# Writing the zeros of a scatter buffer in HBM earlier, from an SBUF region of their own

## The chip, the core and the metric

One Trainium2 core of eight on its chip runs the program; the others are idle. The metric is the device time of one execution in microseconds (us), as a median over runs. Everything is float32 at the borders; inside, many matmuls split a factor into a rounded high part (fp32r) and the low rest, so that one product is three matmuls.

## The reference

Three blocks act on x, 8 x 64 tokens of 512 features, with residuals:

```python
x = x + xattn(layernorm(x), ctx_1024, ...)   # scores of 64 tokens against 512 context rows, softmax,
                                             # concat [c, c2q, c*c2q, c*q2c] @ W_l.T + b_l
x = x + attn(layernorm(x), ...)              # qkv, causal attention (16 heads of 32, S = 64),
                                             # conv of width 3 over tokens gives new queries,
                                             # attention again, out projection
x = x + ffn(layernorm(x), ...)               # 14 experts, top 2 of a softmax gate,
                                             # gelu(x @ w1[e] + b1[e]) @ w2[e] + b2[e], weighted sum
```

The last block is sparse here: each token's normed row is scattered to the rows of its two experts in an HBM buffer, each block of 128 rows is multiplied with its expert's weights, and the results are gathered back. Rows of a block that no token fills must hold zeros, so the buffer is cleared first.

## The kernel before

The 512 tokens are four tiles (n = 0..3, NT = 4) of 128 (P). The program is one block with a list of instructions for each engine; the order on an engine is the order in which they are written, and semaphores tie the engines together. There are three stages. The first is the cross attention with its projection, some 106 us long: a loop `for n in range(1, NT)` on ScalarE (ACT), VectorE (DVE) and TensorE (PE), whose pass n finishes the scores of tile n and starts those of tile n + 1 (`exp_scores(n + 1)`). The second is the small attention: `fill` pieces (projections of q, k, v and, later, the convolution) are woven on PE between `scores(m, half)`, `values(m)` (transposes of probabilities) and `outputs(m)`, m = 0..7 being two rounds over the four tiles. The third are the experts, with a loop over pairs of blocks.

What the change touches:

- `rows_dram` is the HBM buffer, 57 blocks (ROW_BLOCKS) of 128 rows of 512 floats: 14,592 KB. It is cleared by one DMA whose source is `zero_rows`, a 128 x 512 tile of zeros read 57 times. Before, `zero_rows` is another name for `att`, the tile into which the first stage's `exp_scores` writes and which later holds rows of the scatter's helper matrices (`spread`).
- `zero_made` tells that the tile holds zeros, `rows_zeroed` reaches 16 when the DMA has landed. GpSimd (POOL) fills the tile at L835, once the first stage is over (`z_psum` at NT); ACT issues the DMA at L658 to L661, behind `copy_cT(1, NT - 1)`. DVE waits for `rows_zeroed` ahead of `spread(0)` (L1376, it is the first that overwrites `att`), POOL ahead of the scatter.
- `A2` (its rounded view is `A2r`) is a region that changes its use with the stages. In the second stage, `o_hi` lies at columns 6144 and up: it holds the first attention's outputs with a border of zeros ("pads") that POOL writes at L834; DVE fills it in `take_out(m)` (L1162, and L1170 for the low rest `o_lo`). In the first stage, columns 3584 to 7680 hold the split parts.
- POOL's set-up in the second stage runs from L834 to L840: pads, three iotas (`slot_row_made`, for which DVE waits at L1333), pads of `o_lo`. Behind it stands `norm_probabilities(m)` (L823), for which `values(m)` on PE waits.
- On PE, the fill `("conv", 0, 0)` (L1683 to L1685) waits for `o_low` at 8, that is for the end of `take_out(1)` on DVE, and stands right behind `scores(3, 0)` and `scores(3, 1)` (L1704 and L1715).
- SyncE (SP) issues nearly all other loads. Around the change: context rows of tile 3 (L376), `conv` and `wo` (L402, L403) once the first stage is over, copies of v between halves (L408), then the first experts' weights (L413 to L415).

Of the kernel before, what the change touches and what calls it, by code (L numbers as in the profile page):

```python
# [23 lines left out]
P = 128  # L24
B, S = 8, 64
D = 512
Q = 512
KT = D // P
N = B * S
NT = N // P  # L30
# [7 lines left out]
ROW_BLOCKS = E + E * MORE + 1  # L38
# [10 lines left out]
def perceiver_kernel(nc, t, out):  # L49

    ctx = ExitStack()
    with ctx:
        def sb(name, shape, dt=F32):
            return ctx.enter_context(nc.sbuf_tensor(name, shape, dt))

        def overlaid(name, rounded_name, shape):

            with nc.sbuf_tensor(name, shape, F32) as plain:
                pass
            return plain, sb(rounded_name, shape, F32R)  # L60

        def sem(name):
            return ctx.enter_context(nc.semaphore(name))


        rows_dram = nc.dram_tensor("rows_dram", [ROW_BLOCKS * P, D], F32).ap()
# [60 lines left out]
        last_w = wqkv_flat[:, 4096:4608].rearrange("p (t s) -> p t s", t=NT)  # L127
        last_wT = wqkv_flat[:, 5120:5632].rearrange("p (t n) -> p t n", t=NT)
        A2, A2r = overlaid("A2", "A2r", [P, 3 * KT * N + KT * B * (S + 2)])
        cwT = A2[:, 0:2048].rearrange("p (k n) -> p k n", k=KT)  # L130

        c2qT, ccT, cqT = (A2[:, at:at + D].rearrange("p (k n) -> p k n", k=KT) for at in (2048, 2560, 3072))
# [23 lines left out]
        hpre = A2[:, 2048:3072]  # L156
        hT = A2[:, 3072:5120].rearrange("p (u f n) -> p u f n", u=2, f=FT)
        ysb = A2[:, 5120:6144].rearrange("p (u d) -> p u d", u=2)
        att = sb("att", [P, Q]); zero_rows = att

        attT = sb("attT", [P, KT, P]); c2q = sb("c2q", [P, D])
        slot_row_i = c2q[:, 0:P].bitcast(I32); last_w2 = c2q[:, P:2 * P]
# [110 lines left out]
        zero_made, rows_zeroed = sem("zero_made"), sem("rows_zeroed")  # L273
# [22 lines left out]
        def tile(n):  # L296
            return slice(n * P, (n + 1) * P)
# [8 lines left out]
        def out_bank(w):  # L306

            return TB if w else PO
# [5 lines left out]
        def piece(*what):  # L314

            return FILLS.index(what)
# [6 lines left out]
        def pieces(part, n):  # L323

            return parts_ahead[:, n - 1] if part == 0 and n else parts[:, part]

        def source(part, n):

            return (cT[:, :, tile(n)], c2qT, ccT, cqT)[part]
# [5 lines left out]
        def sixth_hi(i):  # L335

            return qkv_hi[i // 2][:, :, D * (i % 2) // 2:D * (i % 2 + 1) // 2]
# [136 lines left out]
        def _(act):  # L474
# [8 lines left out]
            def copy_cT(l, n):  # L483
                act.wait_ge(cT_psum, NT * l + n + 1)
                nc.scalar.activation((c_hi if l == 1 else cT)[:, :, tile(n)], turn_bank(l, n)[:, :].rearrange(
                    "p (k n) -> p k n", k=KT), ACT.Copy).then_inc(cT_ready, 1)
# [14 lines left out]
            def high_part(part, n):  # L501

                if part == 0:
                    act.wait_ge(cT_ready, n + 1)
                elif part == 1:
                    act.wait_ge(c2qT_ready, n + 1)
                elif part == 2:
                    act.wait_ge(cc_ready, n + 1)
                    if n:
                        act.wait_ge(z_psum, n)  # L510
                else:
                    act.wait_ge(cqT_ready, n + 1)
                nc.scalar.activation(pieces(part, n)[:, 0], source(part, n), ACT.Copy).then_inc(part_high[part], 1)

            def exp_scores(n):
                act.wait_ge(nmax_ready, n + 1)
                if n:
                    act.wait_ge(aT_psum, n)
                nc.scalar.activation(att[:, :], SC[:, :], ACT.Exp, bias=nmax[:, n:n + 1],
                                     accum_out=asum[:, n:n + 1]).then_inc(exp_done, 1)  # L520

            def turn_weights(n):

                act.wait_ge(aT_psum, n + 1)
                if n:
                    act.wait_ge(cq_psum, n)
                nc.scalar.activation(attT[:, :, :], TR[:, :].rearrange("p (k n) -> p k n", k=KT),
                                     ACT.Copy).then_inc(aT_ready, 1)

            def exp_maxima(n):  # L530

                act.wait_ge(msub_ready, n + 1)
                nc.scalar.activation(mT[:, :, :], mT[:, :, :], ACT.Exp).then_inc(mexp_done, 1)

            def copy_c2qT(n):

                act.wait_ge(c2qT_psum, n + 1)
                nc.scalar.activation(c2qT, TR[:, :].rearrange("p (k n) -> p k n", k=KT),
                                     ACT.Copy).then_inc(c2qT_ready, 1)

            def high_qkv(i):

                if i == 0:
                    act.wait_ge(wqkv_in, 16)
                    act.wait_ge(first_psum, NT)
                elif i == 4:
                    act.wait_ge(z_psum, NT)
                nc.scalar.activation(sixth_hi(i), wqkv[:, :, sixth(i)], ACT.Copy).then_inc(qkv_high, 1)
# [22 lines left out]
            for n in range(1, NT):  # L571
                turn_weights(n)
                high_part(2, n - 1)
                exp_maxima(n)
                if n == 2:
                    for i in range(4):
                        high_qkv(i)
                copy_c2qT(n)
                high_part(1, n)
                high_part(3, n)  # L580
                if n >= 2:
                    copy_cT(1, n - 2)
                if n + 1 < NT:
                    exp_scores(n + 1)
            high_part(2, NT - 1)

            def take(g):
# [55 lines left out]
            def exp_logits(n):  # L643
# [12 lines left out]
            take(2)  # L656
            take(3)
            copy_cT(1, NT - 1)  # L658
            act.wait_ge(zero_made, 1)
            act.dma_start(rows_dram.rearrange("(b p) d -> p b d", p=P),  # L660
                          zero_rows[:, :].unsqueeze(1).to_broadcast([P, ROW_BLOCKS, D])).then_inc(rows_zeroed, 16)  # L661
            take(piece("v", 0))
            exponentials(0)
            take(piece("qk", 1, 0))
# [120 lines left out]
        def _(pool):  # L785
# [21 lines left out]
            pool.wait_ge(consts, CONSTS - 1)  # L807
            nc.gpsimd.iota(over_row_i[:, :], pattern=[[1, OVER]], base=1, channel_multiplier=0).then_inc(consts, 1)

            pool.wait_ge(s_psum, 1)  # L810
            for dst, src in ((qkv_b, "qkv_bT"), (conv_b, "conv_bT")):
                pool.dma_start(dst[:, :], t[src]).then_inc(params_in, 16)
# [15 lines left out]
            for i in range(4, 6):  # L828
                pool.wait_ge(qkv_high, i + 1)
                nc.gpsimd.tensor_tensor(wqkv_lo[:, :, sixth(i)], wqkv[:, :, sixth(i)],  # L830
                                        sixth_hi(i).bitcast(F32), ALU.subtract).then_inc(pool_low, 1)
            pool.wait_ge(z_psum, NT)
            for side in (0, S + 1):
                nc.gpsimd.memset(o_hi[:, :, :, side:side + 1].bitcast(F32), 0.0).then_inc(pads_ready, 1)  # L834
            nc.gpsimd.memset(zero_rows[:, :], 0.0).then_inc(zero_made, 1)  # L835
            nc.gpsimd.iota(slot_row_i, pattern=[[1, P]], base=1, channel_multiplier=0).then_inc(slot_row_made, 1)
            nc.gpsimd.iota(over_e_i, pattern=[[1, E], [0, MORE]], base=0, channel_multiplier=0).then_inc(slot_row_made, 1)
            nc.gpsimd.iota(over_r_i, pattern=[[-1, E * MORE]], base=E * MORE, channel_multiplier=0).then_inc(slot_row_made, 1)
# [50 lines left out]
        def _(dve):  # L889
# [261 lines left out]
            def take_out(m):  # L1151

                n = m % NT
                dve.wait_ge(o_psum, 2 * m + 2)
                for w in range(2):
                    src = out_bank(w)[:, 2 * P * w:2 * P * (w + 1)].rearrange("p (h b s) -> p h b s", h=2, b=2)
                    bias = qkv_b[:, 2 * KT + w:3 * KT:2].unsqueeze(2).unsqueeze(3).to_broadcast([P, 2, 2, S])
                    if m < NT:
                        dst = o_hi[:, w:KT:2, 2 * n:2 * n + 2, 1:S + 1]
                    else:  # L1160
                        dst = cT[:, w:KT:2, tile(n)].rearrange("p h (b s) -> p h b s", b=2)
                    nc.vector.tensor_tensor(dst, src, bias, ALU.add).then_inc(o_ready, 1)  # L1162
                if m >= NT:
                    return
                for w in range(2):
                    dve.wait_ge(o_ready, 2 * m + w + 1)
                    for hp in range(2):
                        k, b = w + 2 * hp, 2 * (n % 2)
                        at = 2 * P * w + P * hp
                        nc.vector.scalar_tensor_tensor(  # L1170
                            o_lo[n // 2][:, k, b:b + 2, 1:S + 1],
                            out_bank(w)[:, at:at + P].rearrange("p (b s) -> p b s", b=2),
                            qkv_b[:, 2 * KT + k:2 * KT + k + 1],
                            o_hi[:, k, 2 * n:2 * n + 2, 1:S + 1].bitcast(F32), ALU.add, ALU.subtract).then_inc(o_low, 1)

            def low_conv(i):

                dve.wait_ge(conv_high, i + 1)
                tap, ks, tiles = conv_half(i)
                nc.vector.tensor_tensor(conv_lo[:, tiles, :], conv[:, tiles, :], conv_hi[tap][:, ks, :].bitcast(F32),  # L1180
                                        ALU.subtract).then_inc(conv_low, 1)
# [156 lines left out]
            sums(1)  # L1338
            add_out_bias(1)
            low_conv(1)  # L1340
            take_out(0)
            low_conv(2)
            softmax(2)
# [29 lines left out]
            finish(2)  # L1373
            choose(1)
            take_counts(0)
            dve.wait_ge(rows_zeroed, 16)  # L1376
            spread(0)
            place(0)
            finish(3)
# [669 lines left out]
```

## Time and profile before

| | |
|---|---|
| runs, us | 459.16, 456.41, 456.44; median 456.44 |
| profiled execution, us | 456.98 |
| its span, first to last instruction, us | 455.4 |
| around the span, us | 1.6 |
| PE busy | 418.7 us (92%) |
| DVE busy | 320.1 us (70%) |
| ACT busy | 195.1 us (43%) |
| POOL busy | 65.3 us (14%) |
| granted TensorE clock, mean of the span | 0.974 |
| moved by DMA | 116.95 MB |

The times of the profile are microseconds from the first instruction of the span. A stretch "106 to 120" is that part of the span. The first stage ends at about 106, the experts begin at about 250. An idle time is put down to what ended it; "issue" is idle time for which the profile shows nothing that the engine waited for.

### The profile page before, as it was taken

Reading aid. Unit: us, or ns where it says so; the run is one execution under the profiler, and the core shown is the slowest. Engines: PE = TensorE matmul, PEld = TensorE weight load, DVE = VectorE, ACT = ScalarE, POOL = GpSimd, SP = SyncE. Lnnn points to the kernel's source line nnn. Section 1 sums busy time; section 2 is a strip of 40 time slices with the busy share of each in tenths; the row PEclk is TensorE's granted clock in tenths of the full one; section 3 lists DMA queues with packets and bytes.
Section 4 is the critical chain, followed back from the end, with each engine's and each line's share of the span. In section 5 each row is a group of like instructions: output and inputs, shape, how many; then the busy total and the mean of one; then the engine's idle time right before and its main releaser. Section 6 shows DMA issues by size and latency. Waiting matters only on the chain.

```text
span 455.4 us, 8169 instructions
## 1 busy us (share of the span) xinstructions
PE 418.7 (92%) x3051; PEld 311.7 (68%) x3060; DVE 320.1 (70%) x605; ACT 195.1 (43%) x347; POOL 65.3 (14%) x80
## 2 busy tenths in 40 slices
PE   1999999999999699999788999999999999999990
PEld 1666566689897598985447756677777777777760
DVE  5759687684379643528866895788887777888637
ACT  4336134223356032233417053676666667765100
POOL 1210000002226110211101600000000000000064
PEclk9999999999999799999879999999999999999997
DMA  7999795005999960029006368999999999994443
GB/s 259 403 390 313 256 417 232 1 1 198 407 407 406 389 251 3 1 90 370 6 4 230 139 231 289 352 358 355 362 386 381 359 348 359 352 338 162 190 140 138
DMA packets 50814, 116.95 MB, mean 257 GB/s; under 512 B 3266, under 2 KB 3282, under 8 KB 50784
## 3 DMA queue, kind: packets, MB, share of 16 engines
q1 hardware_dynamic: 38176, 92.28, 54.7%
q10 hardware_dynamic: 10592, 19.41, 11.2%
q0 software_dynamic: 2016, 4.84, 3.3%
q8 instruction: 21, 0.34, 0.3%
q14 instruction: 9, 0.07, 0.0%
HBM read 93.98 MB, written 21.50 MB: 254 GB/s over the span
## 4 chain that ended last, share of the span: by engine, by line
PE 84%; DVE 7%; issue 3%; ACT 2%; DMA 2%; POOL 1%; DVEq 0%; ACTq 0%; POOLq 0%
PE banks L1943 8%; PE banks L1910 6%; PE banks L1911 6%; PE banks L1912 6%; PE banks L1545 4%; PE banks L1761 3%; PE banks L1546 3%; PE banks L1532 3%; PE banks L1547 3%; PE banks L1584 3%; PE banks L1933 3%; PE banks L1683 3%; PE banks L1685 3%; PE banks L1513 3%; PE banks L1684 3%
## 5 line engine op out<-in xcount | busy, mean ns | idle before, releaser
L1309 DVE TENSOR_TENSOR w_lo<-w,w_hi 128x1024 fp32r<-128x1024 f32 x48 | 55.5, 1218 | 0.0
L640 ACT ACTIVATE w_hi<-w 128x1024 fp32r<-128x1024 f32 x48 | 47.4, 1095 | 1.7 <-DMA w<-in_w 1.7
L723 ACT ACTIVATE A<-banks,b_sb 128x128 f32<-128x128 f32 x112 | 30.5, 384 | 36.3 <-DVE A L1429 20.2
L1910 PE MATMUL banks<-w_hi,cT_r 128*128 128x512 f32 x100 | 40.1, 401 | 0.6 <-DVE cT_r L1326 0.6
L1943 PE MATMUL banks<-w,A 128*128 128x512 f32 x88 | 39.8, 592 | 0.0
L1912 PE MATMUL banks<-w_hi,cT_r 128*128 128x512 f32 x100 | 39.0, 390 | 0.0
L1911 PE MATMUL banks<-w_lo,cT_r 128*128 128x512 f32 x100 | 39.0, 390 | 0.0
L1398 DVE COPY A<-banks 128x512 f32<-128x512 f32 x28 | 18.0, 686 | 16.9 <-PE banks L1912 16.9
L823 POOL TENSOR_TENSOR A<-A,hrec 128x1024 f32<-128x1024 f32 x8 | 17.0, 2129 | 79.3 <-DVE hrec L1149 79.3
L1685 PE MATMUL banks<-A2r,w_lo 128*128 128x256 f32 x96 | 28.1, 293 | 0.0
L871 POOL DMA_DIRECT2D b_sb<-in_b1T x12 | 6.5, 544 | 141.7 <-ACT A L723 134.6
L1943 PEld LDWEIGHTS banks<-w,A 128*128 128x128 f32 x88 | 15.9, 190 | 15.4 <-issue 15.3
L1545 PE MATMUL banks<-w_lo,A2r 128*128 128x512 f32 x52 | 22.5, 433 | 2.1 <-DVE A2r L1007 2.1
L1140 DVE TENSOR_REDUCE hmax<-banks 128x16 f32<-128x1024 f32 x8 | 9.8, 1225 | 18.6 <-PE banks L1715 18.6
L737 ACT ACTIVATE wqkv_lo<-w 128x1024 fp32r<-128x1024 f32 x12 | 12.1, 1052 | 23.7 <-DMA w<-in_w 14.6
L1910 PEld LDWEIGHTS banks<-w_hi,cT_r 128*128 128x128 f32 x100 | 18.8, 188 | 4.4 <-DVE cT_r L1326 0.9
L1761 PE MATMUL banks<-w,cT 128*128 128x512 f32 x32 | 19.2, 755 | 2.5 <-DVE cT L1162 2.5
L1912 PEld LDWEIGHTS banks<-w_hi,cT_r 128*128 128x128 f32 x100 | 18.8, 188 | 4.0
L1546 PE MATMUL banks<-w_lo,A2r 128*128 128x512 f32 x52 | 21.2, 408 | 0.0
L1911 PEld LDWEIGHTS banks<-w_lo,cT_r 128*128 128x128 f32 x100 | 18.8, 188 | 3.4
L1547 PE MATMUL banks<-w_lo,A2r 128*128 128x512 f32 x52 | 21.1, 406 | 0.0
L1659 PE MATMUL banks<-c_hi,w_lo 128*128 128x256 f32 x64 | 18.5, 289 | 0.5 <-DVE A2r L1047 0.5
(332 smaller groups left out, 1027.7 us busy)
## 6 DMA issues: line engine op xcount, KB each, us to landing
w<-in_w SPq DMA_DIRECT2D x24, 2048.0 KB, 10.3
rows_dram<-att ACTq DMA_DIRECT2D x1, 14592.0 KB, 48.7
A<-in_ctxT SPq DMA_DIRECT2D x8, 1024.0 KB, 10.3
A<-in_ctx SPq DMA_DIRECT2D x8, 1024.0 KB, 9.6
w<-in_w SPq DMA_DIRECT2D x5, 1024.0 KB, 6.2
rows_dram<-A ACTq DMA_DIRECT2D x13, 256.0 KB, 6.9
w<-in_wlT SPq DMA_DIRECT2D x3, 1024.0 KB, 14.8
wqkv<-in_wqkvT SPq DMA_DIRECT2D x1, 3072.0 KB, 16.3
```

What stands on the lines that cost most here:

```text
L640: nc.scalar.activation(w1_hi[:, u, k * F:(k + 1) * F], w1[:, u, k * F:(k + 1) * F], ACT.Copy).then_inc(hi_ready, 1)
L723: ins = nc.scalar.activation(hT[:, u, f, :], HT[f // 4][:, tile(f % 4)], ACT.Gelu, bias=b1_sb[:, u, f:f + 1])
L1309: nc.vector.tensor_tensor(w1_lo[:, u, part], w1[:, u, part], w1_hi[:, u, part].bitcast(F32), ALU.subtract).then_inc(lo_ready, 1)
L1545: mm(Z[n][:, :], high[:, k, :], wl_hi[:, at, :], start=(part == 0 and k == 0), stop=False)
L1546: mm(Z[n][:, :], high[:, k, :], wl_lo[:, at, :], start=False, stop=False)
L1547: ins = mm(Z[n][:, :], low[:, k, :], wl_hi[:, at, :], start=False, stop=(part == 2 and k == KT - 1))
L1685: ins = mm(onto, conv_lo[:, KT * tap + k, tile(f)], high, start=False, stop=(tap == CONV_ORDER[-1] and k == KT - 1))
L1761: ins = mm(FB[g % 2][:, :], cT[:, k, tile(n)], wo[:, k, :], start=(k == 0), stop=(k == KT - 1))
L1910: mm(HP[u][c][:, :], xr[:, 0, u, k, :], high[:, at], start=(i == 0), stop=False)
L1911: mm(HP[u][c][:, :], xr[:, 0, u, k, :], low[:, at], start=False, stop=False)
L1912: ins = mm(HP[u][c][:, :], xr[:, 1, u, k, :], high[:, at], start=False, stop=(i == KT - 1))
L1943: mm(onto, hT[:, u, f, :], w2[:, u, f * D + at:f * D + at + width], start=(f == G), stop=False)
```

## The change

The tile of zeros gets columns 7680 to 8191 of `A2`, which nothing uses in the first stage. POOL fills it among its constants at the start. ACT issues the DMA in the loop of the first stage, in the pass n = 2 behind `exp_scores(3)`. As `o_hi` lies over the same columns, POOL waits for `rows_zeroed` ahead of the pads, and DVE ahead of `take_out(0)`; the wait ahead of `spread(0)` goes.

```diff
@@ -127,6 +127,7 @@
         A2, A2r = overlaid("A2", "A2r", [P, 3 * KT * N + KT * B * (S + 2)])
+        zero_rows = A2[:, 7680:8192]
@@ -156,7 +157,7 @@
-        att = sb("att", [P, Q]); zero_rows = att
+        att = sb("att", [P, Q])
@@ -582,6 +583,10 @@
                 if n + 1 < NT:
                     exp_scores(n + 1)
+                if n == NT - 2:
+                    act.wait_ge(zero_made, 1)
+                    act.dma_start(rows_dram.rearrange("(b p) d -> p b d", p=P),
+                                  zero_rows.unsqueeze(1).to_broadcast([P, ROW_BLOCKS, D])).then_inc(rows_zeroed, 16)
@@ -656,9 +661,6 @@
             copy_cT(1, NT - 1)
-            act.wait_ge(zero_made, 1)
-            act.dma_start(rows_dram.rearrange("(b p) d -> p b d", p=P),
-                          zero_rows[:, :].unsqueeze(1).to_broadcast([P, ROW_BLOCKS, D])).then_inc(rows_zeroed, 16)
             take(piece("v", 0))
@@ -807,6 +809,7 @@
+            nc.gpsimd.memset(zero_rows, 0.0).then_inc(zero_made, 1)
             pool.wait_ge(s_psum, 1)
@@ -830,9 +833,9 @@
             pool.wait_ge(z_psum, NT)
+            pool.wait_ge(rows_zeroed, 16)
             for side in (0, S + 1):
                 nc.gpsimd.memset(o_hi[:, :, :, side:side + 1].bitcast(F32), 0.0).then_inc(pads_ready, 1)
-            nc.gpsimd.memset(zero_rows[:, :], 0.0).then_inc(zero_made, 1)
@@ -1338,6 +1341,7 @@
             low_conv(1)
+            dve.wait_ge(rows_zeroed, 16)
             take_out(0)
@@ -1373,7 +1377,6 @@
             take_counts(0)
-            dve.wait_ge(rows_zeroed, 16)
             spread(0)
```

On ACT, in the second stage of before, the DMA stands between the copy of the last normed tile (L485) and the copy of the first v (L593):

```order
L485 ACTIVATE c_hi<-banks 128x4x128 [waits cT_psum]
L660 DMA rows_dram<-att 128x57x512 [waits zero_made]
L593 ACTIVATE A<-banks 128x512 [waits filled]
L611 ACTIVATE A<-w 128x1024 [waits fill_taken,sub_ready]
L604 ACTIVATE A<-banks,qkv_b 128x256 [waits filled]
```

In the changed kernel (later lines have moved by up to 5) it stands in the first stage, between the exponentials of tile 3's scores and the copy of their transposes; `A` is the profile's name for A1 and A2:

```order
L486 ACTIVATE c_hi<-banks 128x4x128 [waits cT_psum]
L520 ACTIVATE att,asum<-banks,nmax 128x512 [waits aT_psum,nmax_ready]
L588 DMA rows_dram<-A 128x57x512 [waits zero_made]
L528 ACTIVATE attT<-banks 128x512 [waits cq_psum,aT_psum]
L514 ACTIVATE A2r<-A 128x512 [waits z_psum,cc_ready]
L534 ACTIVATE mT<-mT 1x128 [waits msub_ready]
```

It moved past all of ACT's work between these two places. On POOL, the set-up of the second stage in before:

```order
L830 TENSOR_TENSOR wqkv_lo<-wqkv,w_lo 128x4x256 [waits qkv_high] x2
L834 MEMSET A2r 128x32 [waits z_psum]
L834 MEMSET A2r 128x32
L835 MEMSET att 128x512
L836 IOTA c2q 128x128
L837 IOTA c2q 128x42
L838 IOTA c2q 128x42
L840 MEMSET cT_r 128x16 x2
L823 TENSOR_TENSOR A<-A,hrec 128x1024 [waits hrec_ready] x2
```

and in the changed kernel:

```order
L833 TENSOR_TENSOR wqkv_lo<-wqkv,w_lo 128x4x256 [waits qkv_high] x2
L838 MEMSET A2r 128x32 [waits rows_zeroed,z_psum]
L838 MEMSET A2r 128x32
L839 IOTA c2q 128x128
L840 IOTA c2q 128x42
L841 IOTA c2q 128x42
L843 MEMSET cT_r 128x16 x2
L826 TENSOR_TENSOR A<-A,hrec 128x1024 [waits hrec_ready] x2
```

The fill with zeros has left this place, and the whole set-up with the first two normalisations stands behind the wait for `rows_zeroed`. On DVE of the changed kernel, the wait for the POOL set-up (`slot_row_made`) and the new one stand here, up to `take_out(0)`:

```order
L1336 CAST before<-c2q 128x128 [waits slot_row_made,dve_step]
L1337 CAST c2q<-c2q 128x42 [waits dve_step]
L1338 CAST c2q<-c2q 128x42 [waits dve_step]
L1143 TENSOR_REDUCE hmax<-banks 128x16 [waits sc_psum,dve_step]
L1144 TENSOR_TENSOR w<-banks,hmax 128x1024 [waits dve_step]
L1183 TENSOR_TENSOR w_lo<-w,cn_hi 128x1024 [waits conv_high]
L1151 TENSOR_REDUCE hsum<-A 128x16 [waits pexp_done]
L1152 RECIPROCAL hrec<-hsum 128x16 [waits dve_step]
L1188 TENSOR_TENSOR x_res<-x_res,ob_row 128x512 [waits normed]
L1183 TENSOR_TENSOR w_lo<-w,cn_hi 128x1024 [waits conv_high,dve_step]
L1165 TENSOR_TENSOR A2r<-banks,qkv_b 128x2x2x64 [waits o_psum,rows_zeroed]
```

The instructions themselves are those of before in the same order; the last row has gained the wait. PE has the same instructions in the same order in both kernels.

## Rows read from the trace of the kernel before

**Rows 1.** The page, part 4: the chain that ended last, by engine.
```profile
PE 84%; DVE 7%; issue 3%; ACT 2%; DMA 2%; POOL 1%; DVEq 0%; ACTq 0%; POOLq 0%
```

**Rows 2.** Waits of PE, 60 to 240: us in total, times, longest.
```profile
PE banks L1715 <- issue: 4.3, 1, 4.3
```

**Rows 3.** Timeline of PE: start, us, instruction, idle time before in brackets.
```profile
148.44 1.46 PE L1715 MATMUL banks<-A 32*64 32x64 f32 x61
154.22 0.47 PE L1715 MATMUL banks<-A 32*64 32x64 f32 x3 [4.31 <-issue]
```

**Rows 4.** Windows, PE: stretch, length, busy (instructions), granted clock, DMA share, GB/s.
```profile
77.00:106.00 29.00, 28.49 (x149) 1.00 0.00 1
...
148.50:151.91 3.41, 1.32 (x62) 1.00 1.06 405
151.91:155.32 3.41, 1.10 (x6) 0.50 1.04 390
155.32:158.74 3.42, 3.42 (x18) 0.50 1.02 364
...
175.80:179.20 3.40, 2.86 (x109) 1.00 0.02 5
...
216.76:220.17 3.41, 1.85 (x72) 1.00 0.04 11
220.17:223.59 3.42, 2.94 (x4) 0.50 0.00 0
...
247.48:250.90 3.42, 2.30 (x24) 1.00 0.06 20
```

**Rows 5.** The page, part 6: DMA issues, KB, us to landing.
```profile
rows_dram<-att ACTq DMA_DIRECT2D x1, 14592.0 KB, 48.7
...
w<-in_convT SPq DMA_DIRECT2D x1, 3072.0 KB, 10.5
```

**Rows 6.** Timeline of DVE.
```profile
126.22 1.81 DVE L1333 CAST before<-c2q 128x128 f32<-128x128 int32 x1
...
131.29 1.23 DVE L1140 TENSOR_REDUCE hmax<-banks 128x16 f32<-128x1024 f32 x1 [2.82 <-PE banks L1715]
...
149.64 0.69 DVE L1162 TENSOR_TENSOR A2r<-banks,qkv_b 128x256 fp32r<-128x256 f32 x2
150.25 1.12 DVE L1170 SCALAR_TENSOR_TENSOR cT_r<-banks,qkv_b,A2r 128x128 fp32r<-128x128 f32 x4
154.73 1.23 DVE L1140 TENSOR_REDUCE hmax<-banks 128x16 f32<-128x1024 f32 x1 [3.37 <-PE banks L1715]
```

**Rows 7.** The chain in order of time: start, us, what.
```profile
134.22 0.87 PE banks L1724 x8
...
154.69 0.51 PE banks L1683
161.03 0.87 PE banks L1724 x8
...
166.28 0.79 PE banks L1745 x53
```

**Rows 8.** Timeline of ACT.
```profile
76.75 0.19 ACT L519 ACTIVATION_READ_ACCUMULATOR att<-banks,nmax 128x1 f32 x1
79.71 0.60 ACT L527 ACTIVATE attT<-banks 128x512 f32<-128x512 f32 x1 [2.76 <-PE banks L1513]
...
116.24 0.41 ACTq L660 DMA_DIRECT2D rows_dram<-att  x1
119.87 0.60 ACT L593 ACTIVATE A<-banks 128x512 f32<-128x512 f32 x1 [3.78 <-PE banks L1669]
...
127.16 2.01 ACT L628 ACTIVATE cn_hi<-w 128x1024 fp32r<-128x1024 f32 x2
```

**Rows 9.** Timeline of SP's queue.
```profile
106.12 0.37 SPq L402 DMA_DIRECT2D w<-in_convT  x1
```

**Rows 10.** Timeline of POOL.
```profile
115.56 0.23 POOL L834 MEMSET A2r<- 128x32 f32 x2
...
125.72 2.22 POOL L823 TENSOR_TENSOR A<-A,hrec 128x1024 f32<-128x1024 f32 x1 [8.87 <-DVE hrec L1149]
```

## The prediction

> **What bounds the kernel now.** I read the page first: the chain that ended last is 84% PE [rows 1], so what counts is work on PE and what keeps it from working. The list of PE's waits comes next. From the middle of the first stage to the gate, PE has one wait of size: 4.3 us ahead of a matmul of L1715, and it is put down to "issue", to nothing that a semaphore or a DMA of the program shows [rows 2]. PE's timeline places it: scores(3, 1) stops three matmuls before its end, at 148.44 + 1.46 = 149.90, and goes on at 154.22 [rows 3]. The windows over PE show two things about it. The DMA engines are full there (share 1.06, 405 GB/s), and the granted clock is at 0.50, which is 1.2 GHz and not 2.4, from 151.91 to 158.74, right after the idle time began [rows 4]. What fills the DMA engines are the zeros: issued at 116.24, landed 48.7 us later, at about 165 [rows 5, 8]. From 77 to 106, where the change puts them, DMA share is 0.00 [rows 4].
>
> What can stop an engine that waits for nothing in the program is its own instructions: they come by DMA too. The dense places test this. In 175.80 to 179.20 PE starts 109 matmuls, again small ones, at a DMA share of 0.02, and is busy 2.86 of 3.40 us; a hole of 4 us has no room there [rows 4]. So I take the 4.31 us to be a page of PE's instructions that came late behind the zeros' packets. It is an inference: dense code under full DMA stalled once, dense code under idle DMA did not.
>
> The Trainium skill ("Runtime: NRT & Kernel Launch", Instruction fetch mechanics) speaks against it: the sequencer fetches the next block of 256 instructions while it runs the present one, and this is said to be hidden, with room for 2048 instructions on PE. By that rule the hole isn't a fetch, and moving the zeros gives 0 instead of 3 to 5 us. The row of the hole, which nothing in the program explains, weighs more for me; the rule feeds a rival below.
>
> **The change, part by part.**
>
> *The hole goes.* scores(3) then ends at about 150.1 (149.90 and the rest, three matmuls). But what follows, the first half fill of the convolution, started at 154.69 [rows 7] and also waits for take_out(1) on DVE. DVE had ended that at 150.25 + 1.12 = 151.37 [rows 6], unseen, because PE was late anyway. From there to PE's first matmul I take 0.1 us (0 to 0.3). So the fill starts at 151.45 and not at 154.69: 3.2 us, and PE is still idle for about 1.4 us, now behind DVE. If the page needs somewhat longer than no time, up to 1.4 us is hidden behind this same wait.
>
> *The low clock.* The half fill from 154.69 took until 161.03, 6.34 us; the next, at 161.03 + 0.87 = 161.90, took until 166.28, 4.38 us [rows 7]. The difference, 2.0 us, is what 1.2 GHz cost. Does it still fall? Before it fell at 151.91, PE had been idle for 2.0 us; before it fell at 220.17, for 1.6 us out of the 3.4 from 216.76 (busy 1.85); with 1.1 us idle from 247.48 to 250.90 (busy 2.30) it stayed at 2.4 GHz there [rows 4]. The changed kernel keeps about 1.4 us of idle time behind small matmuls, which lies between the last two and nearer to the one that fell, so it may go either way. If it falls, I expect it for one stretch as at 220.17 to 223.59, because PE works on without a break: 3.4 us at half speed lose 1.7 us. So the clock gives 2.0 - 1.7 = 0.3 or all 2.0.
>
> *What follows moves along.* From 154 on, PE runs into the next pieces that are released by ACT, DVE or PE; the transfers that matter there (experts' weights) are issued behind PE's progress and move with it. The first three weight loads are issued before the hole and land earlier without the zeros. I take the whole rest as shifted.
>
> *When the zeros land now.* Issue is behind 76.75 + 0.19 = 76.94, so at 77.4 with the 0.41 us of the issue [rows 8]. ACT's next instruction starts at 79.71 after 2.76 us idle, which hides the issue; even if ACT stood as long as it may have at 116.24 (its next record is at 119.87, 3.63 us later), it would be 0.9 us late in front of a copy that is not next in line on PE. 14,592 KB are 14.94 MB; at 405 GB/s [rows 4] this is 36.9 us. First bytes some 2 us behind the issue, my estimate from conv: 10.5 us for 3.15 MB, which are 7.8 us at 405 GB/s, so up to 2.7 [rows 5]. From 79.4 until conv gets going at about 108 (issued 106.12, [rows 9]) 28.6 us move 11.6 MB; 3.35 MB remain. Shared evenly with conv (3.15 MB) this takes 2 x 3.35 / 0.405 = 16.5 us: both landed at about 124. The bounds: zeros first, 116; zeros at a third, 126.
>
> *What waits for that.* conv is needed at 127.16 by ACT's high parts [rows 8]; at 124 it is hidden with 3 us over. POOL's set-up took 115.56 until 125.72 - 8.87 = 116.85, 1.3 us with the fill of att [rows 10]; it now starts at 124 and ends at 125, and norm_probabilities(0) was released at 125.72 by DVE: hidden. The cover, if it is gone: values(0) needs it only at 134.22 [rows 7, 10]. DVE's cast at 126.22 needs the iotas of the set-up; if the zeros land behind 125.3 it is late, and softmax(1) at 131.29 stands behind it, but DVE was idle for 2.82 us ahead of that [rows 6]. So a landing up to 128 costs nothing. take_out(0) stands much later; the new wait there and the one removed cost nothing. The fill of the tile at POOL's start lies in its idle time.
>
> *PE's pages in the new place.* From 77 to 106 PE starts 149 matmuls in 29 us, 5 per us [rows 4]; in the dense place 61 start in 1.46 us, 42 per us [rows 3]. A page that is as late as before, 4 to 7 us, is covered eight times as long there. So I charge 0, with an upper bound of 4.3 us if the hole finds another place.
>
> The sum: 3.2 + 0.3 = 3.5 us with one stretch of low clock, 3.2 + 2.0 = 5.2 without. Against the profiled execution of 456.98 (span 455.4 and 1.6 around it) this is 453.5 or 451.8. That execution lies 0.5 above the median of 456.44, so I take the gain from the median: **452.9**, or 451.2.
>
> **The rivals.**
> - *A: the clock does not fall* (0.25): 451.2. For it: only 1.4 us of idle time remain, little more than the 1.1 us that did nothing. Against it: 1.6 us did, at 216.76.
> - *B: the hole is not made by the zeros* (0.16), or is instead filled by another late page: dense code is enough, or the skill's rule holds. Then 456.4, within 0.5.
> - *C: the clock stays low as long as it did before* (0.07), from 151.91 to 158.74, 6.8 us: another 1.7 us lost, 454.6.
> - *D: slower, the zeros land late* (0.08). If they moved only as in before, 48.7 us from issue [rows 5], and conv and wo (4.2 MB, 10.4 us) went first, they would land at 77.4 + 48.7 + 10.4 = 136.5. Then POOL's set-up ends the iotas at about 137.3, DVE's cast is 11 us late, 2.8 are absorbed ahead of softmax(1) and about 1 later, and take_out(1) ends 7 us late, at 158.6: the fill starts 4 us later than before, 460.4. It decides from a landing at about 132, where the DVE wait has eaten the 3.2 us. For it: DVE and POOL now stand behind the zeros. Against it: the zeros have 28 us of empty DMA.
> - The likeliest (0.40): the hole goes, one stretch of low clock: 452.9. Its own range is 452.2 to 453.7. Some 0.04 is left for what I don't see.
>
> **How the numbers follow.** A measurement of this kernel can tell about 1% (4.6 us) from no change, so faster by over 1% is below 451.9. That is rival A and a little of the likeliest: 0.30. Slower by over 1% (above 461.0) is the bad end of D: 0.04; the rest, 0.66, is within 1%. The range 450.8 to 456.8 holds A, the likeliest, C and most of B (0.84); D is outside.
>
> **What the next profile would show.** The wait "L1715 <- issue" gone or under 1 us; the first convolution matmul at about 151.5 in place of 154.7, right behind the end of DVE's take_out(1); the granted clock low for one stretch at about 152 or not at all; DMA full from 79 to 124 and nearly empty from 125 to 150; POOL's pads at about 124; conv's landing in 14 to 18 us and not 10.5. I am wrong if the hole stands where it stood at idle DMA, if a hole of several us appears between 79 and 124, or if DVE shows a wait for POOL's iotas of more than 2.8 us.

## The result, and the profile after

Over five runs each, in turn on one chip, the changed kernel took 453.8 us (453.66 to 454.06) and the kernel before 456.44 us (454.47 to 459.16). The ratio is 0.9936, with a 95% interval of 0.9917 to 0.9956: 2.0 to 3.8 us less, under 1%. The profiled execution took 453.73 us (before: 456.98), its span is 452.1 us (before: 455.4). The forecast was 452.9, in a range of 450.8 to 456.8.

PE's waits from 60 to 240, which before had 4.3 us at L1715 [rows 2], now have this in their place (us in total, times, longest); L1686 is the first matmul of a convolution fill, L1683 of before:

```profile
PE banks L1780 <- ACT cT L486: 2.5, 2, 1.2
...
PE banks L1686 <- issue: 1.5, 1, 1.5
```

PE's timeline at the place (start, us, instruction, idle time before), against [rows 3]:

```profile
148.28 1.47 PE L1718 MATMUL banks<-A 32*64 32x64 f32 x64
151.28 0.36 PE L1686 MATMUL banks<-A2r,cn_hi 128*128 128x256 f32 x1 [1.53 <-issue]
```

All 64 small matmuls of scores(3) run through: the idle time of 4.31 us in their midst, called the hole below, is gone. PE then idles 1.53 us and starts the fill at 151.28, where before it was 154.69 [rows 7]. DVE's timeline there, against [rows 6]:

```profile
149.46 0.69 DVE L1165 TENSOR_TENSOR A2r<-banks,qkv_b 128x256 fp32r<-128x256 f32 x2
150.07 1.11 DVE L1173 SCALAR_TENSOR_TENSOR cT_r<-banks,qkv_b,A2r 128x128 fp32r<-128x128 f32 x4
151.10 1.21 DVE L1143 TENSOR_REDUCE hmax<-banks 128x16 f32<-128x1024 f32 x1
```

take_out(1) ends at 150.07 + 1.11 = 151.18, and PE starts 0.1 us later. DVE's 3.37 us of idle time ahead of the next reduction are gone. The windows over PE (stretch, length, busy, granted clock, DMA share, GB/s), against [rows 4]:

```profile
77.00:106.00 29.00, 28.49 (x150) 1.00 1.05 406
...
122.00:148.00 26.00, 25.61 (x395) 1.00 0.22 66
148.50:151.70 3.20, 1.58 (x67) 0.97 0.79 192
151.70:155.10 3.40, 3.40 (x18) 0.52 1.03 423
216.70:223.60 6.90, 6.60 (x9) 0.53 0.00 0
```

The zeros fill the DMA engines from 77 on, PE is as busy from 77 to 106 as before (28.49 of 29 us), and at the dense place they are gone (what moves there, 192 GB/s, are mostly the first experts' weights). The clock falls for one stretch at 151.7 and not for two. The issues and landings, against [rows 5, 8, 9], from the page, the list of DMA issues and the timelines of ACT, SP and POOL:

```profile
rows_dram<-A ACTq DMA_DIRECT2D x1, 14592.0 KB, 45.6
...
w<-in_convT SPq DMA_DIRECT2D x1, 3072.0 KB, 17.5
```

```profile
75.98 0.41 ACTq L588 DMA_DIRECT2D rows_dram<-A  x1
...
105.95 0.37 SPq L403 DMA_DIRECT2D w<-in_convT  x1
106.36 6.83 SPq L404 DMA_DIRECT2D w<-in_woT  x1
...
121.74 0.22 POOL L838 MEMSET A2r<- 128x32 f32 x2 [6.28 <-DMA rows_dram<-A]
...
125.56 2.22 POOL L826 TENSOR_TENSOR A<-A,hrec 128x1024 f32<-128x1024 f32 x1 [3.00 <-DVE hrec L1152]
```

The zeros land at 75.98 + 45.6 = 121.6; POOL waits 6.28 us for them, and is ready 3.0 us before DVE releases its first normalisation. conv takes 17.5 us and not 10.5, and lands at 123.5, ahead of its use at 127.

### The profile page after: what moved, and what is told of

Its sections match the earlier page's. It is cut to its first block, busy times and chain, and to the rows that moved or that the text cites. A ratio compares the mean times of both kernels' runs of the same rounds, so it can differ in the third digit from the quotient of the medians.

```text
span 452.1 us, 8170 instructions
## 1 busy us (share of the span) xinstructions
PE 416.6 (92%) x3051; PEld 310.4 (69%) x3060; DVE 319.9 (71%) x605; ACT 195.2 (43%) x347; POOL 65.6 (15%) x80
## 4 chain that ended last, share of the span: by engine, by line
PE 83%; DVE 9%; issue 3%; DMA 2%; ACT 2%; POOL 1%; DVEq 0%; ACTq 0%; POOLq 0%
PE banks L1946 8%; PE banks L1913 6%; PE banks L1915 6%; PE banks L1914 6%; PE banks L1548 4%; PE banks L1550 3%; PE banks L1535 3%; PE banks L1587 3%; PE banks L1549 3%; PE banks L1936 3%; PE banks L1686 3%; PE banks L1687 3%; PE banks L1688 3%; PE banks L1516 3%; PE banks L1926 3%
## 5 line engine op out<-in xcount | busy, mean ns | idle before, releaser
L1764 PE MATMUL banks<-w,cT 128*128 128x512 f32 x32 | 17.8, 708 | 2.5 <-DVE cT L1165 2.5
L624 ACT ACTIVATE A<-banks 128x512 f32<-128x512 f32 x16 | 8.7, 596 | 24.1 <-PE banks L1727 24.1
## 6 DMA issues: line engine op xcount, KB each, us to landing
rows_dram<-A ACTq DMA_DIRECT2D x1, 14592.0 KB, 45.6
```

## The experiments

Twelve kernels ran, each beside the kernel before on its chip. Times are medians; each ratio is to the kernel before in the same call.

**The changed kernel again.**

> The changed kernel once more, on the chip and in the rounds of the two kernels with take_out(1) earlier. Theory (the hole of 4.3 us was a page of PE's instructions that came late behind the zeros; now PE waits 1.5 us for take_out(1) instead, and the clock falls for one stretch): 453.5 to 454.1, 2.4 to 3.5 us under the kernel before. Rival (the gain of 2.6 us is scatter between executions): within 1 us of the kernel before.

453.94 us against 456.7, ratio 0.9933 (0.9912 to 0.9953), as expected, and in its profile the same 1.5 us at L1686 and no hole. The gain is 2.6 to 3.1 us in both comparisons.

**take_out(1) ahead of sums(2), in the changed kernel and in the kernel before.**

```diff
             low_conv(3)
-            sums(2)
             take_out(1)
+            sums(2)
             softmax(3)
```

> The changed kernel with take_out(1) ahead of sums(2) on DVE, so that the low parts for which conv(0, 0) waits are ready 1.4 us earlier. Theory (the 1.5 us that PE still idles at 149.75 are this wait): the idle time falls to 0.1 to 0.4 us, the clock does not fall at 151.7, so 1.3 + 1.7 = 3.0 us less than the changed kernel: 450.8. Rival (the remaining 1.5 us put down to issue are the rest of a late page): no change, 453.8. Rival (sums(2) now late, values(2) waits for the normalised probabilities): 453 to 454, with a wait of PE ahead of values(2).

> The kernel before with take_out(1) ahead of sums(2). Theory: nothing, 456.4 within 0.5, since there the late page holds PE until 154.2 and take_out(1) has long ended. Rival (DVE was the bound in before too): 453 to 455.

In the changed kernel: 451.15 us, ratio 0.9865 (0.9843 to 0.9887), 2.8 us under the changed kernel beside it. PE's and DVE's timelines (this execution's stages begin 1.2 us later than in the kernel after):

```profile
149.48 1.48 PE L1718 MATMUL banks<-A 32*64 32x64 f32 x64
151.14 0.36 PE L1686 MATMUL banks<-A2r,cn_hi 128*128 128x256 f32 x1 [0.19 <-issue]
...
149.93 1.11 DVE L1173 SCALAR_TENSOR_TENSOR cT_r<-banks,qkv_b,A2r 128x128 fp32r<-128x128 f32 x4
```

The windows over PE:

```profile
148.50:151.70 3.20, 2.77 (x118) 1.00 0.57 106
151.70:155.10 3.40, 3.40 (x31) 1.00 0.89 351
```

The idle time falls from 1.53 to 0.19 us, and the clock no longer falls at 152, so that the first half fill takes 4.61 us (151.14 to 155.75) and not 6.10: 1.3 and 1.5 us, where 1.3 and 1.7 were expected. So what the profile calls "issue" at L1686 is the wait for take_out(1). In the kernel before the same swap brings nothing: 457.28 against 456.7, ratio 1.0018 (1.0000 to 1.0036), with the hole still in place:

```profile
148.99 1.46 PE L1715 MATMUL banks<-A 32*64 32x64 f32 x61
155.13 0.48 PE L1715 MATMUL banks<-A 32*64 32x64 f32 x3 [4.67 <-issue]
```

The second release was covered by the first, and shows only when that is gone.

**The zeros from the old buffer, but later.** The DMA moves in the kernel before:

```diff
             copy_cT(1, NT - 1)
-            act.wait_ge(zero_made, 1)
-            act.dma_start(rows_dram ..., zero_rows ...).then_inc(rows_zeroed, 16)
             take(piece("v", 0))
...
             take(piece("v", 3))
+            act.wait_ge(zero_made, 1)
+            act.dma_start(rows_dram ..., zero_rows ...).then_inc(rows_zeroed, 16)
             exponentials(3)
```

> The kernel before with the same DMA of zeros from att, but issued behind the copy of the last v (about 148) instead of at 116: the DMA engines are idle from 125 to 149 and full from 150 to about 194. Theory (a late page behind the zeros makes the hole, in dense code alone): no hole at 149.9 but the 1.5 us wait for take_out(1), and a new hole of 0.5 to 3 us in or behind the dense place outputs(3), scores(4), at 174 to 182; 453.5 to 456.5. Rival (the dense code alone makes the hole): it stays at 149.9 with 4 us, 456.4. Rival (the zeros hurt only where they stood at 116 to 165 for another reason, by ACT's issue or the POOL fill): 453.8 and no new hole.

453.9 us, ratio 0.9931 (0.9907 to 0.9955): the whole gain of the change, with none of its other parts. No new buffer, no earlier issue, no waits moved. Windows and PE's timeline:

```profile
126.00:148.00 22.00, 21.61 (x360) 1.00 0.11 26
...
173.00:180.00 7.00, 6.11 (x157) 1.00 1.05 405
```

```profile
174.63 1.48 PE L1715 MATMUL banks<-A 32*64 32x64 f32 x64
179.21 0.39 PE L1683 MATMUL banks<-A2r,w_lo 128*128 128x256 f32 x1 [0.36 <-issue]
```

With idle DMA engines up to 148 the hole at 149.9 is gone. In the other dense place, 174 to 179, with DMA full at 405 GB/s, PE runs all 64 small matmuls of scores(4) through and loses 0.36 us three microseconds later, less than the 0.5 to 3 us expected. So full DMA and dense code do not make a hole of several us wherever they meet. What more it takes, the next runs ask.

**More instructions ahead on PE.** In the kernel before, n instructions at the start of PE's program, each of which adds 1 to a semaphore nobody waits for. If the hole stands at a border, the place in PE's program where one block of fetched instructions ends and the next begins, it has to move with them:

```diff
+            for _ in range(16):        # 16, 40, 64, 96
+                pe.sem_inc(padding, 1)
             pe.wait_ge(consts, CONSTS)
```

> The kernel before with 16 more instructions at the start of PE's program, each of which only adds 1 to a semaphore that nobody waits for. Theory (the hole is a page border of PE's instructions, reached before the next page is there): the border moves 16 instructions, that is 8 pairs of weight load and matmul, ahead; PE stops after 53 of the 64 small matmuls of scores(3) and no longer after 61, for 3.6 to 5 us; 456 to 457.5. Rival (the hole belongs to that matmul or its data): it stays after 61.

> The kernel before with 40 more semaphore instructions at the start of PE's program. In the run with 96 of them the first matmul came 8.3 us later and the rest of the program lost nothing more, so one costs about 0.16 us and PE's idle 7.4 us ahead of the first matmul hold 40. Theory (page border): PE stops after about 41 of the 64 small matmuls of scores(3), the page is asked for at about 143 instead of 147, so the hole shrinks from 4.3 to 5 us to 1 to 2.5 us, the first convolution matmul comes at 151.4 to 152.5: 452 to 454.5, that is as good as the changed kernel without moving the zeros. Rival (the whole effect of the 96 was the shift of the program against the zeros or the clock): the hole keeps 4 to 5 us, 456 to 457.5.

> The kernel before with 64 more semaphore instructions at the start of PE. Theory of the border: the hole comes after 29 of the 64 small matmuls of scores(3). Of its length: with 0, 16 and 40 more it was 4.3, 5.0 and 4.9 us, with 96 it was gone. If the page comes at a time of its own, about 153 to 154 whatever the border, the hole is 4.5 to 6 us long and the time 458 to 460 (some 3 us of it because 64 of them are more than PE's idle time at the start); if the lead counts after all, it is 1 to 3 us and the time 455 to 457.

> The same with 96 more instructions. Theory: the border moves 48 pairs ahead, to about the 13th small matmul of scores(3), and the page behind it is asked for at about 142 instead of 147, in slow code. The 7 us that the page took under the zeros (from about 147 to 154.2) are then nearly covered: a hole of 0 to 1.5 us at about 148.7, the first convolution matmul at 151.3 to 151.8 behind take_out(1), 453.5 to 454.7. Rival (the hole is where it is because of data or a semaphore): it stays after 61 matmuls with 4.3 us, 456.5.

PE's timeline at scores(3), with 16, then 40, then 64 more:

```profile
148.58 1.34 PE L1716 MATMUL banks<-A 32*64 32x64 f32 x53
154.94 0.69 PE L1716 MATMUL banks<-A 32*64 32x64 f32 x11 [5.02 <-issue]
```

```profile
147.67 1.16 PE L1716 MATMUL banks<-A 32*64 32x64 f32 x41
153.69 0.92 PE L1716 MATMUL banks<-A 32*64 32x64 f32 x23 [4.86 <-issue]
```

```profile
150.62 0.68 PE L1716 MATMUL banks<-A 32*64 32x64 f32 x29
151.87 1.08 PE L1716 MATMUL banks<-A 32*64 32x64 f32 x35 [0.57 <-issue]
```

PE stops after 53, 41 and 29 of the 64 matmuls, where it was 61 without: 8, 20 and 32 less, exactly half of 16, 40 and 64, since each of these matmuls is a weight load and a matmul. The stop is tied to a count of instructions and not to an operation, its data or a semaphore. With 96 more the border lies after 13; PE runs through all 64, and its only waits there are 0.8 us for a copy of v and 0.65 us ahead of the convolution:

```profile
156.33 0.85 PE L1746 MATMUL banks<-A 64*32 64x64 f32 x64 [0.82 <-DMA A<-A]
...
157.65 1.48 PE L1716 MATMUL banks<-A 32*64 32x64 f32 x64
159.77 0.36 PE L1684 MATMUL banks<-A2r,cn_hi 128*128 128x256 f32 x1 [0.65 <-issue]
```

The medians, against which 456 to 457.5, 452 to 454.5, 455 to 457 or 458 to 460, and 453.5 to 454.7 had been expected in this order, are 458.02 (ratio 1.0013, 0.9993 to 1.0034) with 16, 457.03 (0.9999, 0.9980 to 1.0019) with 40, 456.49 (0.9993, 0.9966 to 1.0021) with 64 and 461.24 (1.0090, 1.0059 to 1.0122) with 96. In the last, PE's first matmul comes at 15.82 instead of 7.35, 8.5 us later, which the expectation had left out; 457.5 + 8.5 = 466 would be the time without any other gain, so 4.8 us came back once the hole was gone. With 64 the first matmul is at 10.94, 3.6 us late, and 4.4 us came back (456.49 where 457.33 + 3.6 would be 460.9); 1.4 us of them were made good before the hole's place, since scores(3) starts at 150.62 and only 2.2 us later than before.

The place of the stop went as the theory said. Its length did not: I had it shrink with the lead that the page gets, and it is 4.3, 5.0, 4.9, 0.6 and 0 us for 0, 16, 40, 64 and 96.

**The instruction packets.** The page, part 3, has a DMA queue of kind "instruction" (packets, MB, share of 16 engines; the same line in every profile):

```profile
q8 instruction: 21, 0.34, 0.3%
```

Its 21 packets have 16 KB each, and the traces hold their times, though no view prints them. This is the one around scores(3) in every profile that has the hole (us; the kernel before if nothing else is said):

| run | packet, start to end | PE goes on at | behind the packet's end |
|---|---|---|---|
| before | 151.82 to 152.71 | 154.22 | 1.51 |
| take_out(1) first | 152.76 to 153.64 | 155.13 | 1.49 |
| 16 more | 152.55 to 153.44 | 154.94 | 1.50 |
| 40 more | 151.35 to 152.22 | 153.69 | 1.47 |
| 64 more | 149.59 to 150.47 | 151.87 | 1.40 |
| weights later (below) | 152.15 to 153.03 | 154.51 | 1.48 |

The stop ends 1.4 to 1.5 us behind the end of the packet, whether it is 0.6 or 5.0 us long. Where there is no hole, the packet was in time: it ended at 146.65 in the changed kernel, 146.42 with the zeros later, and 153.64 with 96 more, while PE comes to the border at about 149.5, 149.4 and 157.9. The 0.36 us at 179.21 with the zeros later are a small stop of the same kind: the third packet behind this one ended at 177.79, 1.42 us before PE went on. So the hole is a block of instructions that comes late. The packet itself takes no longer under the zeros (0.88 to 0.89 us in the table); it starts late, at 149.6 to 152.8. In the five profiles without extra instructions in which PE comes to this place at its usual time and the DMA engines have room ahead of it, it starts at 145.0 to 146.6.

**The changed kernel with 40 more on PE.** The same loop in the changed kernel.

> The changed kernel with the 40 semaphore instructions. Theory (a border in dense code costs only while the zeros are under way): no hole in scores(3), the 1.5 us wait for take_out(1) as before, 453.5 to 454.5. Rival (the changed kernel has its border by luck at a harmless place): a hole of 1 us or more after 41 matmuls, 454.5 to 457.

453.04 us over three runs, a little under the 453.5 to 454.5 expected, ratio 0.9896 (0.9852 to 0.9941):

```profile
147.93 1.47 PE L1719 MATMUL banks<-A 32*64 32x64 f32 x64
150.95 0.36 PE L1687 MATMUL banks<-A2r,cn_hi 128*128 128x256 f32 x1 [1.54 <-issue]
```

With the border 20 pairs further forward there is no hole either. It is not luck of the border's place that the changed kernel is free of it; the packet ended at 144.50, 4.4 us before PE came to the border at 148.9.

**The first weights later, the zeros as before.** In the kernel before:

```diff
             sp.wait_ge(filled, piece("v", 3) + 1)
+            sp.wait_ge(sub_ready, 4)
             first = [t["w1"][u]...
```

> The kernel before, but SP issues the first three loads of experts' weights only when DVE has taken scores(3) (sub_ready at 4), some 4 to 7 us later than at 150. It separates what makes the page late at the border: the zeros alone, or the zeros together with these loads, whose issue begins at 150.1 in the middle of the hole. Zeros alone: the hole stays at 61 of 64 matmuls with 3.5 to 5 us, and the loads come at 157 instead of 150; 456.5 to 457.5. Both needed: a hole under 1.5 us, 453.5 to 454.5.

```profile
148.31 1.46 PE L1716 MATMUL banks<-A 32*64 32x64 f32 x61
154.51 0.48 PE L1716 MATMUL banks<-A 32*64 32x64 f32 x3 [4.74 <-issue]
...
157.60 0.37 SPq L414 DMA_DIRECT2D wqkv<-in_w  x1
```

The hole is there with 4.74 us while the weights' loads come at 157.6. The zeros are enough without these loads. The time, 458.31 over runs from 455.5 to 461.8, ratio 1.0024 (0.9989 to 1.0058), doesn't tell more; 456.5 to 457.5 had been expected.

**The zeros of the changed kernel issued later.** The DMA at about 81 (behind `exp_maxima(3)`), and at about 94 (end of the loop's last pass):

```diff
-                if n == NT - 2:
+                if n == NT - 1:        # behind exp_maxima(n), or at the end of the pass
                     act.wait_ge(zero_made, 1)
```

> The changed kernel with the DMA issued one place later on ACT, at about 81 instead of 76. Theory: landing at 126 to 127, POOL's set-up ends up to 1.5 us behind the time at which DVE wants it, DVE's idle 2.8 us take it up: 453.8 as the changed kernel. Rival (every late landing counts): 455.

> The changed kernel with the DMA issued at the end of the first stage's loop, at about 94. Theory (the rival D of the prediction, made to happen): landing at 139 to 145, because conv and wo come in between; DVE waits 13 to 18 us for POOL's iotas, the first convolution matmul comes at 163 to 167; 465 to 472. Rival (DVE and PE catch most of it up): 454 to 460.

From 81: 454.4 us, ratio 0.9933 (0.9913 to 0.9953), the ratio of the changed kernel. But the landing was 49.4 us behind the issue, at 130.5 and not at 126 to 127, and the wait goes through DVE and ACT:

```profile
130.57 0.22 POOL L838 MEMSET A2r<- 128x32 f32 x2 [14.64 <-DMA rows_dram<-A]
...
131.37 1.95 DVE L1336 CAST before<-c2q 128x128 f32<-128x128 int32 x1 [4.89 <-POOL c2q L841]
...
139.13 0.86 PE L1748 MATMUL banks<-A 64*32 64x64 f32 x64 [0.96 <-ACT A L624]
```

PE loses 0.96 us ahead of outputs(0), so the free room ended a little earlier; the ratios can't resolve that, nor tell the expected 453.8 from the rival's 455. From 94: 466.81 us, ratio 1.0202 (1.0167 to 1.0237), inside the expected 465 to 472:

```profile
143.57 0.22 POOL L838 MEMSET A2r<- 128x32 f32 x2 [27.04 <-DMA rows_dram<-A]
...
144.37 1.94 DVE L1336 CAST before<-c2q 128x128 f32<-128x128 int32 x1 [17.28 <-POOL c2q L841]
...
146.28 1.11 PE L1727 MATMUL banks<-ident,A 128*128 128x128 f32 x4 [11.16 <-POOL A L826]
```

DVE waits 17.3 us for POOL's iotas, as rival D had it, but PE is held first by POOL itself: 11.16 us ahead of values(0), for the first normalisation, which stands behind the same wait.

## Why the prediction was right, point by point

- *The hole goes.* Right. That the zeros make it is shown by leaving everything else as it was (453.9 with the zeros later), that it is a border in PE's instruction stream by its moving 8, 20 and 32 pairs for 16, 40 and 64 instructions, and that it is the page of instructions by the instruction packet, which ends 1.4 to 1.5 us before PE goes on in all six profiles with the hole. The packet starts some 6 us later than in the changed kernel (151.82 for 145.77), inside the 4 to 7 us of the prediction.
- *PE's pages in the new place cost nothing.* Right. In 77 to 106 PE is busy for 28.49 us as before. A packet starts later there too, at 103.73 for 100.62 in the kernel before, whose DMA engines are idle, and costs nothing between long matmuls.
- *The comparison with 175.80 to 179.20* was no good evidence, though the conclusion held. I took dense code without a hole under idle DMA as the test. The run with the zeros later has the same code under full DMA and loses 0.36 us there. What decides is where the border lies in the dense code and when its block comes, and I had not thought of it.
- *3.2 us, because take_out(1) is next in line.* Right in mechanism and size. The fill starts at 151.28 for 154.69, 3.41 us, of which 0.17 us is this execution's earlier start (DVE's L1162 of take_out(1) at 149.64 and at 149.46): 3.24 us. The swap of take_out(1) proves the wait.
- *The clock falls for one stretch, 0.3 us net.* Right, with both its terms somewhat too large. The chain in order of time has the transposes behind the first half fill (L1724 before, at 161.03 [rows 7]) at 157.38, 3.65 us earlier; against the 3.41 at the fill this adds 0.24 us. By the 4.61 us that this half fill takes at full clock (take_out(1) first), the low clock cost it 1.7 us before and 1.5 us after, where 2.0 and 1.7 were put; 2.0 came from comparing it with the next half fill.

```profile
151.28 0.36 PE banks L1686
157.38 0.87 PE banks L1727 x8
```

- *The rest moves along.* Only in the sum. The lead was still 3.65 us where PE's out_project(0) starts, at 206.77 for 210.42; then the clock fell for 6.9 us at 216.7 (granted 0.53) where before it was low for 3.4 us from 220.17 [rows 4], out_project(1) took 6.75 us and not 5.12, and 1.6 us of the lead were gone. Before, the next fall came from 230.4 to 237.3, which the changed kernel does not have, and the lead came back to 3.4 us by 241; it is 3.3 us at the end. That the two nearly cancel is luck: neither was in the sum. The rows of this place in the chain, before and after:

```profile
210.42 3.67 PE banks L1761 x8
220.65 5.12 PE banks L1761 x8
```

```profile
206.77 3.67 PE banks L1764 x8
217.00 6.75 PE banks L1764 x8
```

- *The landing at 124, and what waits for it.* Right with small errors: 121.6. The issue came at 75.98, not 77.4: in ACT's timeline it stands beside the exponentials (L520 starts at 75.98 as well) and not behind them. POOL's set-up, DVE's cast and conv were covered as worked out. The price of rival D was about right: worked out were 4.0 us more than before for a landing at 136.5, and a landing 7.0 us later (143.5) cost 9.3 us (466.8 against 457.5) where this would make it 11. But its first victim is values(0) through POOL, which I had named as a cover and not as the limit.
- *Sharing evenly.* conv and the zeros did share evenly (0.82 MB each from 112 to 116). But with the issue at 81 nearly all of conv and wo was moved ahead of the zeros' end: conv landed at 127.8 and wo at 131.3. So an issue 5.1 us later made the landing 8.9 us later, and another 11.7 us (issue at 92.8) made it 13.0. A landing up to 128 was to cost nothing; at 130.5 PE lost 1 us.
- *The number.* From the profiled execution I had 453.5, and 453.73 was measured. I carried the 3.5 us over to the median, 452.9, and it was 453.8. The term that failed is this carrying over: single executions of the kernel before scatter from 454.5 to 459.2, those after from 453.7 to 454.1, and the profiled one of before was 0.5 us above its median. In the profiles of the kernel before and of its versions with take_out(1) first, with 16 more instructions and with the weights later, the hole was 4.3 to 5.0 us; how long it is in the executions that were not profiled was not seen.

Open stays what sets the time at which the packet starts. It does not follow PE's progress alone: under the same zeros it started at 151.8, 152.6 and 151.4 with 0, 16 and 40 more instructions, and at 149.6 with 64. Open too is what PE does in the 1.4 to 1.5 us behind its end. The best version of these runs is the changed kernel with take_out(1) ahead of sums(2), 451.15 us, 1.35% under the kernel before.

## What to carry to other kernels

An idle time of several microseconds on a busy engine that the profile puts down to nothing ("issue"), in a run of very short instructions, while a large transfer fills every DMA engine, is worth a test: put some empty instructions ahead and see whether it moves by their number. If it does, move the transfer to where the engine's instructions are long; that it is not on the path says nothing of what it does to the engine. The packets of the instruction queue, where a trace has them, settle it: compare their ends with the time at which the engine goes on. And before counting the whole hole as gain, look for what was released during it, which is next in line; here that kept 1.1 us of the 4.3 and, by the clock, 1.5 more.

## What the runs showed of the hardware

An idle time of 4.3 to 5.0 us on PE that no semaphore ends, tied to a position in its instruction stream, appears with 14.9 MB of zeros in flight at 405 GB/s and not with DMA nearly idle (0.11 to 0.22 busy) ahead of it. It ends 1.4 to 1.5 us behind a 16 KB packet of the instruction queue, which takes 0.9 us but starts some 6 us late. The Trainium skill ("Runtime: NRT & Kernel Launch", Instruction fetch mechanics) calls the fetch of the next block mostly hidden; these traces do not agree for this load.

An issue on SP's queue can itself stand still while another queue's large transfer is under way: wo's took 6.83 us at 106.36 under the zeros, and 0.98 us at 106.53 in the kernel before, where they had not begun. The first loads of weights show it too, in the kernel before (under the zeros) and after (without them):

```profile
150.14 2.17 SPq L413 DMA_DIRECT2D wqkv<-in_w  x1
```

```profile
148.87 0.59 SPq L414 DMA_DIRECT2D wqkv<-in_w  x1
```

A semaphore increment on PE took 0.15 us: with 64 of them ahead the first matmul came at 10.94, with 96 at 15.82, 4.88 us for 32. Some 40 are free here, since PE's first matmul waits until 7.35 anyway (7.31 with 40 of them).
